# Mixture-of-experts layers of a four-layer model: all experts over all queries, or tiles of the queries that chose each expert

## The reference

```python
x = x + xattn(layernorm(x), ctx, ...)          # 1024 x 6404 scores for each of 16 heads
x = x + ffn(layernorm(x), ...)                 # layer 1 runs its experts twice (LOOPS = 2)

# the experts, layer 3 (layers 0 and 1 alike; layer 2 is gelu(x @ up.T) @ down.T with 512 hidden channels)
scores_BSN = einsum('bsd,nd->bsn', x, Wr) + br
_, idx_BSK = top_k(scores_BSN + biases_N, 2)
h_NM2H = einsum('md,ndh->nmh', x_MD, Wl1) + bl1[:, None, :]        # every expert over every query
a_NMH, b_NMH = (h_NM2H[..., :H], h_NM2H[..., H:])
y_NMD = einsum('nmh,nhd->nmd', silu(a_NMH) * b_NMH, Wl2) + bl2[:, None, :]
y_MD = einsum('mn,nmd->md', ew_MN, y_NMD)                          # ew is zero but for the two chosen
```

## Time and profile before

| what | us |
|---|---|
| median of 3 runs | 4366.84 |
| lowest and highest | 4354.51 and 4367.82 |
| the profiled execution, its own time | 4359.73 |
| its span (first to last instruction) | 4358.0 |
| PE busy | 4055.6 |
| ACT busy | 3834.7 |
| DVE busy | 2893.0 |
| POOL busy | 587.2 |

### The profile page before, as it was taken

One profiled execution on the slowest core, in us unless ns is written; L12 is line 12 of the kernel. 1 busy time (PEld: TensorE's weight loads), 2 busy tenths in 40 slices (PEclk: granted clock), 3 DMA queues, 4 the chain that ended last, 5 costly groups with the idle time before them and its releaser, 6 DMA issues.

```text
span 4358.0 us, 71738 instructions
## 1 busy us (share of the span) xinstructions
PE 4055.6 (93%) x27834; PEld 1089.2 (25%) x27834; DVE 2893.0 (66%) x6026; ACT 3834.7 (88%) x4271; POOL 587.2 (13%) x545
## 2 busy tenths in 40 slices
PE   7899999999999999999999999899999999999997
PEld 2122222222222222222222222223122232222223
DVE  6889888788987788777603232111686778988833
ACT  3699998989999899888998888889999888999994
POOL 3000002220022211323221101000000000011100
PEclk7699999999999999999999999999999999999998
DMA  5211001000001110010001111011000000000000
GB/s 147 70 28 36 25 25 31 21 21 18 13 20 39 37 36 26 26 31 22 27 23 42 47 35 53 24 35 37 14 15 20 18 24 17 13 16 18 11 14 22
DMA packets 112813, 130.33 MB, mean 30 GB/s; under 512 B 27912, under 2 KB 75024, under 8 KB 112400
## 3 DMA queue, kind: packets, MB, share of 16 engines
q1 hardware_dynamic: 111744, 125.27, 10.3%
q10 hardware_dynamic: 720, 0.40, 0.0%
HBM read 102.24 MB, written 23.34 MB: 29 GB/s over the span
## 4 chain that ended last, share of the span: by engine, by line
PE 61%; ACT 17%; DVE 14%; issue 3%; POOL 0%; DMA 0%; ACTq 0%; SPq 0%; POOLq 0%; DVEq 0%
PE av L1243 25%; ACT prob L1399 13%; PE scores L1233 12%; DVE mpart L1507 10%; PE side L1265 8%; PE scores L1340 6%; PE side L1353 4%; DVE above L1511 3%; PE side L1340 1%; PE scores L1256 1%; ACT above L1409 1%; PE side L1233 1%; PE scores L1380 1%; PE scores L1376 1%; ACT ag L1461 0%
## 5 line engine op out<-in xcount | busy, mean ns | idle before, releaser
L1399 ACT ACTIVATE prob<-scores 128x1024 f32<-128x1024 f32 x2999 | 2905.0, 1032 | 189.9 <-PE scores L1233 98.3
L1507 DVE TENSOR_REDUCE mpart<-side 128x1 f32<-128x512 f32 (+1 forms) x3456 | 2075.9, 655 | 391.6 <-PE side L1265 381.5
L1243 PE MATMUL av<-prob,VB 128*9 128x512 f32 x6528 | 871.6, 607 | 0.6 <-ACT prob L1399 0.5
L1243 PE MATMUL av<-prob,VA 128*9 128x512 f32 x6528 | 863.5, 601 | 1.7 <-ACT oS L1419 0.8
L1265 PE MATMUL side<-KA,QP 32*128 32x512 f16 (+1 forms) x2112 | 596.5, 393 | 66.9 <-DVE mpart L1507 40.7
L1233 PE MATMUL scores<-QP,KA 32*128 32x512 f16 x2998 | 579.9, 389 | 38.9 <-ACT prob L1399 23.1
L1265 PE MATMUL side<-KB,QP 32*128 32x512 f16 (+1 forms) x2112 | 551.5, 381 | 60.0 <-DVE mpart L1507 32.9
L1233 PE MATMUL scores<-QP,KB 32*128 32x512 f16 x3000 | 575.9, 387 | 30.5 <-ACT prob L1399 16.5
L1511 DVE CUSTOM_DVE_ANT_0 above<-side,above 128x512 f32<-128x512 f32 x768 | 503.5, 686 | 116.9 <-PE side L1265 100.6
L1409 ACT ACTIVATE above<-scores 128x1024 f32<-128x1024 f32 x384 | 395.4, 1030 | 61.7 <-DVE mpart L1511 41.9
L1233 PEld LDWEIGHTS scores<-QP,KB 32*128 32x128 f16 x3000 | 138.7, 91 | 776.3 <-ACT prob L1399 642.4
(11 more groups left out here) (196 smaller groups left out, 2316.9 us busy)
## 6 DMA issues: line engine op xcount, KB each, us to landing
KA<-kstacks SPq DMA_DIRECT2D x384, 48.0 KB
KB<-kstacks SPq DMA_DIRECT2D x384, 48.0 KB
Fin<-in_Fin SPq DMA_DIRECT2D x64, 256.0 KB, 2.6
kstacks<-hi SPq DMA_DIRECT2D x100, 128.0 KB, 2.4
ctxc<-in_ctxT SPq DMA_DIRECT2D x36, 256.0 KB, 3.0
hT<-in_mask SPq DMA_DIRECT2D x16, 400.2 KB, 3.5
kstacks<-lo SPq DMA_DIRECT2D x50, 128.0 KB, 2.5
Fout<-in_Fout SPq DMA_DIRECT2D x48, 128.0 KB, 2.7
```

The source lines that it names most:

```text
L1243: last = pe.matmul(AV[ROWS * h:ROWS * h + VC, :], V[l % 2][:, kt, g * HG + h, :], prob[:, (e + h // 2) % RING, (h % 2) * QB:(h % 2) * QB + ...
L1399: act.activation(prob[:, e % RING, :], pair.rearrange("p a b -> p (a b)"), ACT.Exp if softmax(l) else ACT.Sigmoid, scale=SCALE).then_inc(s ...
L1507: dve.tensor_reduce(part, bank, AX.X, ALU.max).then_inc(sem["red"], 1)
```

## The change

A pass now computes an expert only for the queries that chose it. The 1024 choices of a unit's 512 queries (two each) are ranked by expert on the chip: DVE makes a slot number for each ("routec", "slota" to "slotc"), with the first slot of each expert at a multiple of 128. With 8 experts this needs at most 1024 / 128 + 7 = 15 tiles of 128 slots (ST), and always 15 are computed. POOL scatters the rows of the normed queries to these slots in a DRAM buffer ("scat", 8 transfers by index), SP loads them back as tiles ("xload", 4 transfers), and PE turns them ("gT"). For each tile POOL fetches the rows of the expert that it belongs to with two transfers by index ("win", "wout", 30 in a pass, a ring of 6). "up" is now four 128-column matmuls in one block, "down" is 2 (layer 2: 4) matmuls of 128 columns, and their result goes through DVE ("yc") and SP ("yput") to a second DRAM buffer, from which POOL gathers each query's two rows ("yget", 8 transfers by index) for DVE to add ("ysum", eight). In layers 0 and 1 (but for unit 3) ACT copies all of a tile's hidden channels at once ("agc"), in layer 3 DVE does with the bias. The planner's third pair of banks ends at phase 20 instead of near the end of phase 22, and its table of costs has entries for the new steps.

```diff
-W_RING = 3
+W_RING = 6
+W_LEN = 516
 H_RING = 4
-BIAS_AT = 2
+GELUS = 3
+HID_RING = 2 * GELUS
+
+ST = 2 * QB // P + E - 1
+SLOTS = ST * P
+FOURS = [range(i, min(i + 4, ST)) for i in range(0, ST, 4)]
...
-WIDE = (15, 8), (22, KT - 4)
+WIDE = (15, 8), (20, 0)
...
+def behind(l):
+
+    return 1 if FFN[l]["gated"] else GELUS + 1
+
+
...
+def fetches_of(u, lp):
+
+    n = behind(unit(u)[0])
+    return [(w, (u, lp, k)) for j in range(ST + n) for w, k in (("win", j), ("wout", j - n)) if 0 <= k < ST]
...
+def weights_used(what, key):
+
+    return ("down" if what == "wout" else "agc" if unit(key[0])[0] == 3 else "up"), key
+
+
+def fetch_before(what, key):
+
+    i = FETCHES.index((what, key))
+    return weights_used(*FETCHES[i - W_RING]) if i >= W_RING else None
...
-    out = [Step("SP", "wexp", (u, lp, k)) for k in range(W_RING)] + [Step("PE", "logit", (u, lp))]
...
-    def gated(k, j):
-        a, g = Step("PE", "up", (u, lp, k, j)), Step("PE", "up", (u, lp, k, n + j))
-        if by_dve(u, lp) and l == 1:
-            return [a, Step("DVE", "ac", (u, lp, k, j)), Step("ACT", "tanh", (u, lp, k, j)), g, Step("DVE", "gc", (u, lp, k, j)),
-                    Step("DVE", "gatea", (u, lp, k, j)), Step("DVE", "gateb", (u, lp, k, j))]
-        out = [a, Step("ACT", "tanh", (u, lp, k, j)), Step("ACT", "ac", (u, lp, k, j)), g]
...
-        return out + [Step("ACT", "gc", (u, lp, k, j)), Step("POOL", "gatea", (u, lp, k, j)), Step("POOL", "gateb", (u, lp, k, j))]
...
+    n = behind(l)
+    by = "DVE" if by_dve(u, lp) or l == 3 else "ACT"
+    fetch = deque(Step("POOL", w, k) for w, k in fetches_of(u, lp))
+    out = [Step("PE", "logit", (u, lp))]
+    out += [Step("DVE", what, (u, lp)) for what in ("routea", "routeb", "routee", "routef", "routeg", "routec", "routeh")]
+    out += [Step("PE", "count", (u, lp))]
+    out += [Step("DVE", what, (u, lp)) for what in ("slota", "slotb", "slotc", "slotd")]
+    out += [Step("ACT", "rexp", (u, lp))]
+    out += [Step("DVE", what, (u, lp)) for what in ("routej", "routek", "routel", "routed")]
+    out += [Step("POOL", "scat", (u, lp, c)) for c in range(2)]
+    out += [Step("SP", "xload", (u, lp, i)) for i in range(len(FOURS))]
+    out += [fetch.popleft() for i in range(W_RING)]
+    if l == 3:
+        out += [Step("PE", "cwT", (u, lp)), Step("ACT", "cwTc", (u, lp)), Step("PE", "bias", (u, lp)), Step("DVE", "badd", (u, lp))]
+
+    def turned(i):
+        return [Step("PE", "gT", (u, lp, i)), Step("ACT", "gTc", (u, lp, i))]
+
+    def next_fetch():
+        return [fetch.popleft()] if fetch else []
+
+    out += turned(0)
+    for j in range(ST + n):
+        if j < ST:
+            if j % 4 == 2 and j // 4 + 1 < len(FOURS):
+                out += turned(j // 4 + 1)
+            out.append(Step("PE", "up", (u, lp, j)))
+            if f["gated"]:
+                out += [Step(by, "agc", (u, lp, j)), Step("ACT", "tanh", (u, lp, j))]
+            else:
+                out.append(Step(by, "upc", (u, lp, j)))
+            out += next_fetch()
+        if j >= n:
+            k = j - n
+            out += [Step("PE", "down", (u, lp, k)), Step("DVE", "yc", (u, lp, k))]
+            out += next_fetch()
+            if k % 4 == 3 or k == ST - 1:
+                out.append(Step("SP", "yput", (u, lp, k // 4)))
+        if j < ST:
+            if f["gated"]:
+                out += [Step("DVE" if by_dve(u, lp) else "POOL", what, (u, lp, j)) for what in ("gatea", "gateb")]
+            elif j % GELUS == GELUS - 1 or j == ST - 1:
+                out += [Step("ACT", "gelu", (u, lp, k)) for k in range(j - j % GELUS, j + 1)]
+    assert not fetch
+    out += [Step("POOL", "yget", (u, lp, c)) for c in range(2)]
+    out += [Step("DVE", "ysum", (u, lp, c)) for c in range(2)]
...
+                elif s.what == "gT":
+                    u, lp, i = s.key
+                    bank = bank_free("gT", u, lp, i)
+                    own.wait_ge(*o.sem("xload", u, lp, i))
+                    for t, j in enumerate(FOURS[i]):
+                        last = pe.transpose(bank[:, t * P:(t + 1) * P], xg[:, j, :], ident[:])
+                    last.then_inc(sem["bgP"], 1)
...
-                    pe.matmul(bank[0:fs, :], Fin[:, w, j * fs:(j + 1) * fs], xnT[:], start=True, stop=True).then_inc(sem["bgP"], 1)
...
+                    for i in range(4):
+                        last = pe.matmul(bank[0:fs, i * P:(i + 1) * P], W[:, w, i * fs:(i + 1) * fs], xgT[:, j * P:(j + 1) * P], start=True, stop=True)
...
-                    for t in range(QT):
-                        last = pe.matmul(bank[:, t * P:(t + 1) * P], h[:, t * P:(t + 1) * P], Fout[0:fs, w, c, :], start=c + t == 0, stop=(c, t) == (nk - 1, QT - 1))
...
+                    for c in range(nk):
+                        last = pe.matmul(bank[:, 0:D], h[:, c * P:(c + 1) * P], W[0:fs, w, c * D:(c + 1) * D], start=c == 0, stop=c == nk - 1)
...
+                elif s.what == "slotc":
...
+                    places = cnt[:, 0:QT * E].rearrange("p (t e) -> p t e", e=E)
+                    of_each = tmp[:, 0:2 * QT * E].rearrange("p (c t e) -> p c t e", c=2, e=E)
+                    v.did(dve.scalar_tensor_tensor(sel[:], broadcast(base[:].unsqueeze(1), full), float(P), places, ALU.mult, ALU.add))
+                    v.did(v.after().tensor_tensor(of_each, oh[:], broadcast(sel[:].unsqueeze(1), [P, 2, QT, E]), ALU.mult))
+                    v.did(v.after().tensor_reduce(slf[:].rearrange("p (c t) -> p c t", c=2), of_each, AX.X, ALU.add))
+                    v.did(v.after().tensor_copy(slot[:], slf[:]))
...
+                elif s.what == "scat":
+                    u, lp, c = s.key
+                    own.wait_ge(*o.sem("slotc", u, lp))
+                    own.wait_ge(*(o.sem("weight", u, f"r{lp}") if unit(u)[0] == 1 else o.sem("scale", u, "f")))
+                    if pass_before(u, lp):
+                        for i in range(len(FOURS)):
+                            own.wait_ge(*o.sem("xload", *pass_before(u, lp), i))
+                    for t in range(QT):
+                        to = bass.IndirectOffsetOnAxis(ap=slot[:, QT * c + t:QT * c + t + 1], axis=0)
+                        pool.indirect_dma_start(xslot, to, xn[:, t, :], None).then_inc(sem["d_scat"], 16)
+                elif s.what in ("win", "wout"):
+                    u, lp, j = s.key
+                    w, f = o.wslot[s.what, s.key], FFN[unit(u)[0]]
+                    n = 4 * f["fs"] + 4 * (unit(u)[0] == 3) if s.what == "win" else f["nk"] * D
+                    own.wait_ge(*o.sem("slotd", u, lp))
+                    if fetch_before(s.what, s.key):
+                        used, k = fetch_before(s.what, s.key)
+                        own.wait_ge(*o.sem(used, *k))
+                    at = bass.IndirectOffsetOnAxis(ap=widx[:, j:j + 1], axis=0)
+                    pool.indirect_dma_start(W[:, w, 0:n], None, A[f"{s.what}{unit(u)[0]}"], at).then_inc(sem[f"d_w{w}"], 16)
+                elif s.what == "yget":
+                    u, lp, c = s.key
+                    own.wait_ge(*o.sem("slotc", u, lp))
+                    own.wait_ge(*o.sem("yput", u, lp, len(FOURS) - 1))
+                    for t in range(QT):
+                        at = bass.IndirectOffsetOnAxis(ap=slot[:, QT * c + t:QT * c + t + 1], axis=0)
+                        pool.indirect_dma_start(y12[:, QT * c + t, :], None, yslot, at).then_inc(sem[f"d_yget{c}"], 16)
...
+                elif s.what == "xload":
+                    u, lp, i = s.key
+                    own.wait_ge(*o.sem("scat", u, lp, 1))
+                    own.wait_ge(*o.sem("qadd", u - 1, NG - 1))
+                    if pass_before(u, lp):
+                        own.wait_ge(*o.sem("yput", *pass_before(u, lp), len(FOURS) - 1))
+                    four = slice(FOURS[i][0], FOURS[i][-1] + 1)
+                    sp.dma_start(xg[:, four, :], xslot.rearrange("(j p) d -> p j d", p=P)[:, four, :]).then_inc(sem[f"d_xload{i}"], 16)
+                elif s.what == "yput":
+                    u, lp, i = s.key
+                    own.wait_ge(*o.sem("yc", u, lp, FOURS[i][-1]))
+                    four = slice(FOURS[i][0], FOURS[i][-1] + 1)
+                    sp.dma_start(yslot.rearrange("(j p) d -> p j d", p=P)[:, four, :], xg[:, four, :]).then_inc(sem["d_yput"], 16)
```

More of the change, by code:

```diff
@@ L270, in __init__ @@
                     ring.insert(0, 2)
-            if s.eng == "SP":
+            if s.what in DMAS:
                 name, k = self.dma_name(s), 16 * (DMAS[s.what] + self.more(s))
@@ new lines, in steps_before @@
+    if w in chain:
+        return [(chain[w], key)]
+    if w == "routed":
+        return [("routel", key), ("slota", key)]
+    if w in ("win", "wout"):
+        return [("slotd", (u, lp))] + [x for x in [fetch_before(w, key)] if x]
+    before = pass_before(u, lp)
+    if w == "scat":
+        return [("slotc", (u, lp))] + ([("xload", (*before, len(FOURS) - 1))] if before else [])
+    if w == "xload":
```

(18 more changed lines are left out.)

548 lines of the change are left out of this document (262 added, 286 removed).

## The result

The changed kernel takes 4208.07 us (median of four runs, 4205.49 to 4210.31) against 4361.96 for the kernel before (median of its four): a ratio of 0.9648, 95% interval 0.9629 to 0.9667. The forecast was 4216. The profiled execution took 4205.49 us, its span is 4203.8: 154.2 less than the execution profiled before.

The account below looks back on a forecast made before the run. The prediction took PE, busy 93% of the span, to bound the kernel. From 4359.7 us it took 186 for saved PE work, added 15 for waits and 27 for the tail: 4216 us, range 4145 to 4315.

Parts of the forecast that it names:

- PE sets the pace: Attention units 0 to 6: PE bounds them, so 220 us less PE work makes them 186 us shorter.
- Half shows: Rival, attention: ACT and DVE catch hold first, only 110 us of the saving shows, 4292 us; chance 0.17.
- PE's conversion: Attention: time per us of experts' PE work, about one for one in units 0, 1, 5; 0.6 and 0.65 in 3, 4.
- The 15 us for new waits: Attention: 15 us allowed in all for waits in nine passes that the planner's table got wrong.
- near nothing: Sign, attention: PE's wait for the first turn and DVE's for the gathered rows would be near nothing.
- x: POOL's queue: time that one transfer by index holds POOL, taken as 1.3 us.
- The rival that VectorE holds up each issue: POOL's queue: one DVE instruction of 0.7 us delays each issue, 2.0 us a transfer, 4246 us in all; chance 0.13.
- The Trainium skill's rule on that: GpSimd can't write descriptors during VectorE's two-port fast mode; a 620 ns transfer took 3100 ns; not added to the sum.
- The tail: After the attention: grows from 77.7 to 105.2 us, a loss of 27.5 us.
- The sum's two branches: Tail length: 84.4 + 16x us while the tiles set the pace, 42.3 + 46x us when POOL does.
- The slack: Attention: nothing stops PE or DVE at x = 1.3; from x = 2.2 each us more costs about 16 us a pass.
- slower than before: Rival: transfers by index cost POOL far more, 4487 us at x = 3.5, deciding near x = 2.8; chance 0.08.

Follow-up runs that it names:

- up_quarter_b: Repeat, on another chip, of the changed kernel with only the first of four matmuls issued in each block going up: 4172.46 us.
- later_u2: Changed kernel with the pace of unit 2's two passes stretched, last blocks due 16 key tiles later (196 instead of 180): 4201.08 us.
- wide_back: Changed kernel with the scores' ring of three pairs of banks kept to the end of phase 22 instead of phase 20: 4221.15 us.
- dose_one_b: Repeat of the changed kernel with one POOL power of 128x4 (1.04 us) ahead of each transfer by index: 4399.58 us.
- dose_planned: Changed kernel with one POOL power ahead of each transfer by index, and the planner's costs raised to 2.3 us a transfer: 4248.81 us.

## Why the prediction was right, and where it was wrong

**PE sets the pace: right before the change, half right after it.** PE's work in the units was forecast to fall by 220 us; it fell by 206.8, and 182.9 of that showed, 0.88 of it, against 186 forecast. Blocks cost what was taken, in the median: up 1.09, down 0.64 (0.65 taken), a turn 0.59 (0.56). "Half shows" is ruled out for the change itself. But the next 73 us that up_quarter_b took off PE gave only 36. The conversion is not a constant: it falls as PE comes down to ACT. PE and ACT stood at 3411.8 and 3282.6 us before, at 3205.0 and 3195.0 after. ACT's own 88 us less got no value in the sum. No run takes only PE's share from the kernel before, so 0.88 is what both together gave, and how much of it PE's share would have given alone isn't known.

One reading in the prediction was wrong. It took PE's conversion as 0.6 in unit 3 and 0.65 in unit 4, from 139 and 89 us of PE work that stand in no row. By the busy times of the earlier trace rows PE works 88.6 us longer in unit 3 than in four phases like 31, for 82.7 us of time, and 54.8 longer in unit 4 than in three phases like 31 and one like 7, for 58: near one to one, as in the other units. So the "half shows" rival had no support there, and unit 3 then gave 39.6 us for 33.7 of PE's time.

**By unit, the sizes were off and nearly cancelled.** Units 0, 1, 3 and 5 came at -25, -21, -40, -38 for 21, 21, 35, 31 forecast. Unit 2 gave 25 of 42, because its second pass was squeezed into phase 14 (later_u2 gets 17 of it back). Unit 4 gave -2 of 18 and unit 6 gave 36 of 18: the maxima for layer 3 moved forward. Of the matmuls "max" (L1265 before, L1318 now) unit 4 has 51 more, unit 5 has 21 fewer and unit 6 has 30 fewer. In phase 22 DVE is busy 64.7 us now and 36.3 before (windows 2883.1 to 3004.7 and 3000.8 to 3115.2), and wide_back shifts the same time back (33.9). The forecast took each unit's maxima as fixed.

**The 15 us for new waits.** On PE they were too many: at turns and downs 2.2 us. On DVE the sign "near nothing" failed. Its waits for the gathered rows in the changed kernel's units, from zs and xs, the queries' state:

```profile
DVE zs L1810 <- DMA y<-yslot,slot: 29.5, 6, 8.9
DVE xs L1810 <- DMA y<-yslot,slot: 25.9, 4, 8.8
```

That is 55.4 us in ten waits: the 21 us between the last "yput" and the last add that the prediction counted in key tiles were not there in five of the nine passes. They fall in phases 15, 17, 19, 22 and 31, where no maxima, or few, stand behind them. PE's waits for DVE's maxima (mpart, both lines) are 80 us against 73 before, so little of it reached PE, and the rest was hidden by where it fell, not by the slack that was forecast.

**Transfers by index: x = 1.27 for 1.3.** The bound that was taken, POOL's own gate over 128 rows, was near by luck as much as by reason: no run shows why 0.96 and 0.30. The rival that VectorE holds up each issue (x = 2.0) is out: the 150 fetches of input weights have a mean of 0.99 us with DVE busy 68% of the time. The Trainium skill's rule on that (page "SBUF — State Buffer", section "SBUF: two separate sides") isn't seen at work here; DVE's long instructions read PSUM, and whether one in a two-port mode would do it no run shows.

**The tail.** 30.1 for 27.5. The sum's two branches hold up: 105 at x = 1.27 (measured 105.6 and 107.8), 42.3 + 46x = 147 at 2.28 (149.9) and 198 at 3.38 (200.4).

**The slack: this step was wrong.** The prediction said that nothing stops PE or DVE up to x = 2.2. At x = 2.28 each pass lost 16 us. The first scatter, the load back and the first turn of unit 0's pass in the changed kernel, timeline:

```profile
688.24 1.22 POOL L1900 DMA_INDIRECT xslot<-xn,slot  x1 [19.70 <-DVE slot L1713]
...
699.59 3.06 SPq L2032 DMA_DIRECT2D slots<-xslot  x4
...
707.54 0.66 PE L1392 MATMUL side<-ident,slots 128*128 128x128 f32 x4
```

The way from scatter to turn is 19.3 us here, not the 23 that nine key tiles were taken for, as the first scatter starts only when DVE's slot numbers come (the wait in its row); in the other eight passes it is 16.4 to 19.8. And a load back of 256 KB lands in 4.9 us (median), not in 2.6 as the weight loads of the earlier trace rows; four go out at once here, but no run shows that this is the reason. 699.59 - 688.24 + 4.9 = 16.3 leaves 3 us for eight scatters: the edge of this pass is near x = 1.65 (an estimate from these rows), and by the same sum the last two passes, with 16.4 us, had next to nothing left. Behind it the six fetches stand on POOL ahead of the first gate, which the sum left out. And since the order is fixed, the other engines come to stand with PE, and its clock is lower after (the 46 us of longer work above), so a late us costs more than one. The rival "slower than before" thus decides not near 2.8 but near 2.1 (an estimate: 2.05 on the line between the changed kernel, 4208.5 at 1.27, and dose_one_b, 4399.6 at 2.28, where it meets 4357 of before, and up to 2.15 if the units lose nothing below 1.65). The forecast was spared this only because x came out at 1.27; that was luck as far as the slack goes. dose_planned shows that the edge lies in the order, not in the engine: planned at 2.3, such transfers cost the units nothing.

## What to carry to other kernels

In these runs work saved on the busiest engine showed almost in full until the next engine's sum was reached: compare the sums per stage before and after, and expect the conversion to fall as they meet. In an order that is laid out from a table of costs, a wrong cost hurts by all engines at once, and the slack is only what the table left: give it the measured cost first (worth 151 us here, 4399.6 to 4248.8), then judge the operation. Read such a slack off the trace, from the instruction that starts the chain to the one that waits, and not in planned steps. Where nothing overlaps, a chain of transfers by index (46 here, 1.27 us each) can cost more than the matmuls that it saves; use such a change only for the stages that hide it.
